# The first six output tiles: x stored early, and the last layer's bf16 result added onto it in DRAM by GpSimd's transfers

## The reference, cut to what matters

```python
x = x + L0_ffn(cond(x))   # ternary weights, 1024 hidden
x = x + L1_ffn(cond(x))   # mixture of experts, top 2 of 8
x = x + L2_ffn(cond(x))   # int8 weights, gate and up, 704 hidden
inputs = cond(x)          # last layer: sigmoid(x) * ratio
h = mx_layernorm(bf16_round(inputs)); h = mx_linear(h, W1, b1)
h = mx_gelu(h);                       h = mx_linear(h, W2, b2)
x = x + bf16_round(bf16_round(inputs) + h)
```

## Time and profile before

| | us |
|---|---|
| median of 3 runs | 413.33 (412.79 to 413.59) |
| profiled execution, its own time | 415.14 |
| its span | 413.4 |
| its mean granted TensorE clock | 0.963 of full speed |

### The profile page before, as it was taken

One profiled execution on the slowest core, in us unless ns is written; L12 is line 12 of the kernel. 1 busy time (PEld: TensorE's weight loads), 2 busy tenths in 40 slices (PEclk: granted clock), 3 DMA queues, 4 the chain that ended last, 5 costly groups with the idle time before them and its releaser, 6 DMA issues.

```text
span 413.4 us, 7058 instructions
## 1 busy us (share of the span) xinstructions
PE 365.5 (88%) x2496; PEld 314.6 (76%) x2507; DVE 337.5 (82%) x495; ACT 288.6 (70%) x513; POOL 90.7 (22%) x107
## 2 busy tenths in 40 slices
PE   3995458779789999999999999999998998999885
PEld 1995445458677889999999999999986787878453
DVE  4999966999885999999999980899404797899986
ACT  5999956996978378757667675766543455778873
POOL 4000300000030153343333332447530000000000
PEclk9998587989996999999999999999999999999999
DMA  7700000000048865411161279381004200000002
GB/s 274 262 2 2 1 0 0 2 0 2 1 131 300 287 195 168 174 39 40 34 246 40 74 273 367 77 304 43 25 27 131 88 0 2 1 2 2 0 27 78
DMA packets 22642, 38.41 MB, mean 93 GB/s; under 512 B 2072, under 2 KB 17064, under 8 KB 22480
## 3 DMA queue, kind: packets, MB, share of 16 engines
q1 hardware_dynamic: 17120, 24.98, 17.6%
q0 software_dynamic: 2480, 6.95, 5.0%
q10 hardware_dynamic: 3008, 6.03, 4.2%
HBM read 32.83 MB, written 5.11 MB: 92 GB/s over the span
## 4 chain that ended last, share of the span: by engine, by line
PE 65%; ACT 16%; DVE 11%; issue 5%; DMA 2%; SPq 0%; ACTq 0%; DVEq 0%
PE bank L1773 20%; PE bank L1813 19%; PE bank L1609 7%; PE bank L1892 3%; PE bank L1643 2%; PE bank L1882 2%; ACT big L494 1%; ACT big L493 1%; DVE big L1304 1%; ACT yT L558 1%; PE bank L1803 1%; DMA v<-in_kT 1%; DMA g<-choice_rows 1%; PE bank L1661 1%; ACT big L570 1%
## 5 line engine op out<-in xcount | busy, mean ns | idle before, releaser
L1813 PE MATMUL bank<-big,yT 128*128 (+1 forms) x368 | 83.6, 380 | 0.0
L639 ACT ACTIVATE yT<-bank,big 128x128 f32<-128x128 f32 x176 | 50.3, 368 | 41.7 <-PE bank L1773 41.7
L1813 PEld LDWEIGHTS bank<-big,yT 128*128 128x128 f32 x368 | 68.0, 190 | 8.7 <-issue 0.4
L392 POOL TENSOR_TENSOR small<-small 128x2 f32<-128x2 f32 (+1 forms) x9 | 9.6, 1071 | 167.9 <-DVE small L1339 71.1
L440 POOL DMA_INDIRECT choice_rows<-yo,rowo x23 | 30.5, 1325 | 61.5 <-ACT yo L648 48.8
L425 POOL DMA_INDIRECT xg<-token_rows,rowi x22 | 32.3, 1469 | 50.0 <-PE bank L1803 28.3
L1773 PE MATMUL bank<-ygT,w3T 128*128 128x128 f32 x256 | 30.2, 276 | 0.6 <-ACT ygT L631 0.6
L1773 PEld LDWEIGHTS bank<-ygT,w3T 128*128 128x128 f32 x256 | 29.8, 192 | 1.1 <-issue 0.7
L1773 PEld LDWEIGHTS bank<-ygT,big 128*128 128x128 f32 x256 | 29.8, 192 | 0.7 <-issue 0.4
L1773 PE MATMUL bank<-ygT,big 128*128 128x128 f32 x256 | 29.9, 275 | 0.0
L1773 PEld LDWEIGHTS bank<-ygT,y 128*128 128x128 f32 x224 | 26.0, 192 | 1.5 <-issue 1.2
(11 more groups left out here) (383 smaller groups left out, 823.8 us busy)
## 6 DMA issues: line engine op xcount, KB each, us to landing
big<-in_moe_w SPq DMA_DIRECT2D x16, 1024.0 KB
v<-in_kT SPq DMA_DIRECT2D x2, 512.0 KB, 4.5
big<-in_gateT SPq DMA_DIRECT2D x1, 1024.0 KB, 6.9
big<-in_upT SPq DMA_DIRECT2D x1, 1024.0 KB, 9.0
big<-in_downT SPq DMA_DIRECT2D x1, 1024.0 KB, 11.2
x<-in_x_bsc SPq DMA_DIRECT2D x1, 1024.0 KB, 13.6
token_rows<-y POOLq DMA_DIRECT2D x4, 256.0 KB, 7.9
ek<-in_w3a ACTq DMA_DIRECT2D x1, 1024.0 KB, 5.8
```

Source lines behind the costliest of these rows:

```text
L392: gp.tensor_tensor(dst, src, pexp[:, 0:dst.shape[1]], ALU.pow).then_inc(dst_sem, 1)
L639: ins = sc.activation(hT[j % 2][:, c], ps[1 + 2 * (j % 2) + c // 4][:, (c % 4) * P:(c % 4 + 1) * P], ACT.Gelu, bias=b1s[:, c, j:j + 1] if ...
L1813: ins = te.matmul(ps[5 + 2 * (j % 2)][:, 0:C], hT[j % 2][:, c], big[:, bass.ds(at + (W2_AT + c * C), C)] if j else big[:, W2_AT + c * C:W2 ...
```

## The change

VectorE no longer adds the bf16 sums of tiles 0 to 5 to x. SP stores x of each of the first three pairs, 256 KB at a time, when `x_l2` says that layer 2 has been added. When all three stores have landed, GpSimd's queue adds the bf16 sums of each pair onto the output in DRAM by a transfer with `accum_op=add`, from bf16 in SBUF to float32 in DRAM. Tiles 6 and 7 are finished and stored as before. `ob` becomes eight tiles, four of them in free columns of `big`, so ScalarE's waits for `x_done` go. SP waits at the end for the two plain stores and the three adding transfers. To stay within the number of semaphores, some that were always waited for together are merged (the waits ask for the sum of the counts).

```diff
@@ SP
-            for i in range(T):
-                sp.wait_ge(s["x_done"], i + 1)
+            for p in range(G - 1):
+                sp.wait_ge(s["x_l2"], p + 1)
+                sp.dma_start(out_v[:, 2 * p:2 * p + 2], x[:, 2 * p:2 * p + 2]).then_inc(s["x_out"], 16)
+            for i in (T - 2, T - 1):
+                sp.wait_ge(s["x_done"], i - T + 3)
                 sp.dma_start(out_v[:, i], x[:, i]).then_inc(s["stored"], 16)
-            sp.wait_ge(s["stored"], 16 * T)
+            sp.wait_ge(s["stored"], 32)
+            sp.wait_ge(s["sum_out"], 16 * (G - 1))
@@ GpSimd, behind the four powers
+            out_v = out.rearrange("b (s p) c -> p (b s) c", p=P)
+            pool.wait_ge(s["x_out"], 16 * (G - 1))
+            for p in range(G - 1):
+                pool.wait_ge(s["sum_ready"], p + 1)
+                gp.dma_start(out_v[:, 2 * p:2 * p + 2], ob_pair[p], accum_op=ALU.add).then_inc(s["sum_out"], 16)
@@ ScalarE
             def copy_ob(i):
                 act.wait_ge(s["d3_ready"], i + 1)
-                if i >= 4:
-                    act.wait_ge(s["x_done"], 2 * (i // 2) - 2)
-                sc.activation(ob[:, i % 4], ps[7][:, 0:C], ACT.Copy).then_inc(s["ob_ready"], 1)
+                sc.activation(ob[i], ps[7][:, 0:C], ACT.Copy).then_inc(s["ob_ready"], 1)
@@ VectorE
             def finish_sum(i):
                 dve.wait_ge(s["ob_ready"], i + 2)
-                mark("sum", ve.tensor_tensor(pair_of(ob, i % 4), pair_of(ob, i % 4), pair_of(res, i), ALU.add))
-
-            def finish_pair(i):
-                after("sum")
-                ve.tensor_tensor(pair_of(x, i), pair_of(x, i), pair_of(ob, i % 4), ALU.add).then_inc(s["x_done"], 2)
+                ve.tensor_tensor(ob_pair[i // 2], ob_pair[i // 2], res[:, i:i + 2], ALU.add).then_inc(s["sum_ready"], 1)
...
-            finish_pair(0)
...
-            finish_pair(2)
...
-            finish_pair(4)
@@ merged semaphores: ld_wgu and ld_wd; w3_copy and r3_copy; w3_copy2 and r3_copy2
```

More of the change, by code:

```diff
@@ L134, in bass_adaln_ffn_stack @@
         q3T = [big[:, 11776 + 512 * j:12288 + 512 * j].bitcast(BF16).rearrange("p (c t) -> p c t", c=HC3) for j in range(2)]
-        ob = big[:, 12800:13312].bitcast(BF16).rearrange("p (t c) -> p t c", t=4)
+        ob = [big[:, at:at + 512].bitcast(BF16).rearrange("p (t c) -> p t c", t=4)[:, j] for at in (12800, 15360) for j in range(4)]
+        ob_pair = [big[:, at:at + 256].bitcast(BF16).rearrange("p (t c) -> p t c", t=2) for at in (12800, 13056, 15360)]
         b1t = big[:, 13312:13824].bitcast(BF16)
@@ L218, in bass_adaln_ffn_stack @@
             table_ready rowo_ready xt_ready xt_copy h1_ready ld_b2
-            yo_ready ld_v1 ld_wgu ld_wd ld_x ld_router ld_l2 ld_l3rows consts iota_done
+            yo_ready ld_v1 ld_wgud ld_x ld_router ld_l2 ld_l3rows consts iota_done
             act_step dve_step pool_step tf_sum tf_ready tf2_ready decay_ready sx_ready ek_raw ek_ready ekv_ready clamped euk_ready
@@ L223, in bass_adaln_ffn_stack @@
             silu_ready z_ready sq2 amax2 rms2_in rms2_pow scale2 q2_magic q2_tr q2T_ready
-            down_ready q2T_last x_l0 sig1 yT_ready rh_ready rh_gelu logits lg_shift lg_exp last_gelu last_sum last_ps last_row  masks_ready             gate_ready gcT_tr gcT_ready ps1_ready ps2_ready bias_ready l1_done             w3q w3t w3_copy l2_int xt2_tr sig2 y2_ready y2h_ready y2T_ready gu2_ready silu2_ready h2_ready down2 x_l2             r3_tr r3_copy sig3 y3_ready var3 pow3 hq3 hq3_tr hq3T u3_ready a3_ready g3_ready q3_ready
-            q3_tr q3T_ready d3_ready ob_ready x_done stored w3_copy2 r3_copy2 bias_added br_ready b1_ready ld_b1 b1_turned b1s_ready w1_ready y1_stored a_ready b_ready rows_ps rows_ready ek_free zero_row""".split()
+            down_ready q2T_last x_l0 sig1 yT_ready rh_ready rh_gelu logits lg_shift lg_exp last_gelu last_sum last_ps last_row  masks_ready             gate_ready gcT_tr gcT_ready ps1_ready ps2_ready bias_ready l1_done             w3q w3t dve_copies l2_int xt2_tr sig2 y2_ready y2h_ready y2T_ready gu2_ready silu2_ready h2_ready down2 x_l2             r3_tr sig3 y3_ready var3 pow3 hq3 hq3_tr hq3T u3_ready a3_ready g3_ready q3_ready
+            q3_tr q3T_ready d3_ready ob_ready x_done stored act_copies bias_added br_ready b1_ready ld_b1 b1_turned b1s_ready w1_ready y1_stored a_ready b_ready rows_ps rows_ready ek_free zero_row sum_ready sum_out x_out""".split()
         s = {n: sem(n) for n in NAMES}
@@ L294, in _ @@
             for m, n in enumerate(("gateT", "upT")):
-                sp.dma_start(wgu[:, m], A[n].rearrange("(k p) h -> p k h", p=P)).then_inc(s["ld_wgu"], 16)
-            sp.dma_start(wd, A["downT"].rearrange("(c p) n -> p c n", p=P)).then_inc(s["ld_wd"], 16)
+                sp.dma_start(wgu[:, m], A[n].rearrange("(k p) h -> p k h", p=P)).then_inc(s["ld_wgud"], 16)
+            sp.dma_start(wd, A["downT"].rearrange("(c p) n -> p c n", p=P)).then_inc(s["ld_wgud"], 16)
             sp.dma_start(x[:], A["x_bsc"].rearrange("b (s p) c -> p (b s) c", p=P)).then_inc(s["ld_x"], 16)
@@ L513, in _ @@
             euk(1)
-            act.wait_ge(s["ld_wgu"], 32)
-            act.wait_ge(s["ld_wd"], 16)
+            act.wait_ge(s["ld_wgud"], 48)
             for m in range(3):
@@ L705, in _ @@
                 act.wait_ge(s["w3t"], b + 1)
-                sc.activation(w3T[:, 1, (b - 2) * 1024:(b - 1) * 1024], ps[b][:].bitcast(BF16), ACT.Copy).then_inc(s["w3_copy2"], 1)
+                sc.activation(w3T[:, 1, (b - 2) * 1024:(b - 1) * 1024], ps[b][:].bitcast(BF16), ACT.Copy).then_inc(s["act_copies"], 1)
             for b in range(2, 4):
                 act.wait_ge(s["r3_tr"], b + 1)
-                sc.activation(r3t[:, 2 * b:2 * b + 2].rearrange("p t c -> p (t c)"), ps[4 + b][:], ACT.Copy).then_inc(s["r3_copy2"], 1)
+                sc.activation(r3t[:, 2 * b:2 * b + 2].rearrange("p t c -> p (t c)"), ps[4 + b][:], ACT.Copy).then_inc(s["act_copies"], 1)
             for b in range(2):
@@ L1262, in _ @@
                 dve.wait_ge(s["w3t"], b + 1)
-                ve.tensor_copy(w3T[:, 0, b * 1024:(b + 1) * 1024], ps[b][:].bitcast(BF16)).then_inc(s["w3_copy"], 1)
+                ve.tensor_copy(w3T[:, 0, b * 1024:(b + 1) * 1024], ps[b][:].bitcast(BF16)).then_inc(s["dve_copies"], 1)
             for b in range(2):
                 dve.wait_ge(s["r3_tr"], b + 1)
-                ve.tensor_copy(r3t[:, 2 * b:2 * b + 2].rearrange("p t c -> p (t c)"), ps[4 + b][:]).then_inc(s["r3_copy"], 1)
+                ve.tensor_copy(r3t[:, 2 * b:2 * b + 2].rearrange("p t c -> p (t c)"), ps[4 + b][:]).then_inc(s["dve_copies"], 1)
             dve.wait_ge(s["br_ready"], 1)
@@ L1323, in norm_in @@
                 dve.wait_ge(s["sig3"], p + 1)
-                dve.wait_ge(s["r3_copy"], 2)
-                dve.wait_ge(s["r3_copy2"], 2)
+                dve.wait_ge(s["dve_copies"], 4)
+                dve.wait_ge(s["act_copies"], 4)
                 ve.tensor_tensor(pair(res, p), y3[p % 2], pair(r3t, p), ALU.mult).then_inc(s["y3_ready"], 1)
@@ L1452, in finish_sum @@
                 dve.wait_ge(s["ob_ready"], i + 2)
-                mark("sum", ve.tensor_tensor(pair_of(ob, i % 4), pair_of(ob, i % 4), pair_of(res, i), ALU.add))
-            def finish_pair(i):
-                after("sum")
-                ve.tensor_tensor(pair_of(x, i), pair_of(x, i), pair_of(ob, i % 4), ALU.add).then_inc(s["x_done"], 2)
+                ve.tensor_tensor(ob_pair[i // 2], ob_pair[i // 2], res[:, i:i + 2], ALU.add).then_inc(s["sum_ready"], 1)
             def tile_sum(i):
                 dve.wait_ge(s["ob_ready"], i + 1)
-                mark(("sum", i), ve.tensor_tensor(ob[:, i % 4], ob[:, i % 4], res[:, i], ALU.add))
+                mark(("sum", i), ve.tensor_tensor(ob[i], ob[i], res[:, i], ALU.add))
             def finish_tile(i):
                 after(("sum", i))
-                ve.tensor_tensor(x[:, i], x[:, i], ob[:, i % 4], ALU.add).then_inc(s["x_done"], 1)
+                ve.tensor_tensor(x[:, i], x[:, i], ob[i], ALU.add).then_inc(s["x_done"], 1)
             dve.wait_ge(s["ld_sgu"], 16)
@@ L1846, in _ @@
             ratio_to_tokens(3, 4, s["r3_tr"])
[L1848 to L1851, removed]
+            pe.wait_ge(s["dve_copies"], 4)
+            pe.wait_ge(s["act_copies"], 4)
             keep_clock(6, 7)
```

## The result

The changed kernel is slightly slower. On 20 runs its median is 415.53 us against 414.18 for the kernel before on the same chips, and the ratio is 1.003 (95% interval 1.0016 to 1.0045): 1.2 us more, where 0.4 us less was forecast. Its own profiled execution took 415.44 us, with a span of 413.7.

The account below looks back on a forecast made before the run. The prediction took the end to be bound by the chain of VectorE's last tile, one store and its landing. Its sum, -0.6 (second addition) + 0.2 (shared engines) = -0.4 us, took 413.33 to 412.9 us, range 412.3 to 415.2.

Parts of the forecast that it names:

- Step (2): Removing VectorE's addition for tiles 2 and 3 lets tile 7's maximum start 0.61 to 0.83 us earlier; taken as 0.6.
- The bound by TensorE: Clock-keeping matmuls ahead of TensorE's turn of tile 6 do not move, limiting that branch's gain to 0.64 us.
- Steps (1), (3) and (4): Removing VectorE's additions for tiles 0/1, for tiles 4/5, and ScalarE's four waits for x: each worth nothing.
- Early stores at nothing: SP's three added 256 KB stores of x cost nothing, covered by the empty DMA.
- The third transfer's latency: GpSimd's adding transfer for tiles 4 and 5: 4.8 us from issue to landing, landing at 412.5.
- The 0.2 us for shared engines: At the end, third adding transfer and last plain store finish together and share DMA engines, adding 0.2 us.
- So the end is this chain: VectorE's last tile, one store, a landing: End of the kernel before: last store issued 411.3, data down about 413.0 of a 413.4 us span.
- three signs of being wrong: Third landing over 6.2 us; SP's last wait for adding transfers by over 0.5 us; early stores shifting work before 399.
- Rival C: Third adding transfer becomes the end, deciding from 5.4 us latency, over 0.8 us slower from 6.2; chance 0.30.
- Rival D: VectorE holds up writing the third transfer's descriptors, making the time 413.5 us; chance 0.06.
- E: The second addition's place ahead of tile 7's maximum stays empty, so no gain, 413.5 us; chance 0.06.
- The 0.27 for "slower": Chance of over 0.2% slower: 0.25 from Rival C's larger part, 0.02 from Rival D and E.

Follow-up runs that it names:

- e8: Kernel before, with room for eight tiles of bf16 sums and the addition for tiles 2 and 3 moved behind tile 7's quantisation; ratio 0.997.
- e9: Kernel before plus the three early 256 KB stores of x, overwritten by the usual stores at the end; ratio 0.9995.
- e7: Changed kernel, but the third GpSimd transfer converts bf16 to float32 without adding, leaving x out of tiles 4 and 5; ratio 1.0002 to the kernel before.

## Why the prediction was wrong

- **Step (2), the gain, was right in mechanism and under-sized.** The maximum could start 0.03 us after the GELU, the upper end of the 0.61 to 0.83 given, and the whole chain moved by 0.8 us, not 0.6. The 0.36 us of "issue" at 401.48 did not stay: in the changed kernel VectorE was idle for 0.15 us at that place (400.35 to 400.50), most of it until the GELU was done, and in e8, where this addition comes long after its sum, nothing like it stands before it. (The addition there is that of tiles 2 and 3, the second, not "the first adding of x".) The bound by TensorE (0.64 us; its own figures, 405.51 - 404.85, give 0.66) failed, because the end of the clock-keeping matmuls that I took (403.82 + 1.03) is a modelled one; the turn started 0.16 us ahead of that end in the changed kernel (403.57 against 402.70 + 1.03).
- **Steps (1), (3) and (4) at nothing: right.** e8 keeps the additions of tiles 0/1 and 4/5 on VectorE and has the full gain. e8 drops ScalarE's waits and so does not test (4), but the rows bear it out: the eviction of tile 6 stood behind TensorE's product for 0.55 us in the kernel before and does so in the changed one.
- **Early stores at nothing: right** (e9).
- **The third transfer's latency was right as a number:** 4.8 us estimated between bounds of 2.4 and 8.1, 4.7 and 4.5 measured. Part of that is luck: it was the middle of two even rates, and the measured transfer began at 47 GB/s. Over all traces, adding transfers took 3.8 to 4.7 us, 3.8 to 4.6 with no store near them. The Trainium skill's fit (DMA: Bandwidth & Descriptors, Anatomy of one DMA) gives an estimate of 3.5 us for 640 KB, read and written bytes together; the measurement says more for an adding transfer. For e7, which only converts, the fit's estimate is 2.9 us for the 384 KB read and written and 2.6 us for the 256 KB written; the trace has 2.6.
- **The 0.2 us for shared engines was too small.** The last store landed in 2.4 instead of 1.7 us, so 0.7, and e7 shows that the adding does it. With this and the gain, SP was done 11.3 us after the GELU (411.8 - 400.47), against 11.4 before (413.0 - 401.59). Gain and sharing alone would have made no difference.
- **The step that failed is "So the end is this chain: VectorE's last tile, one store, a landing".** It gave the end 0.4 us behind the last landing, whatever queue that came from. GpSimd's own closing drain, 2.2 us behind the landing of its last transfer and at least 4.1 behind its last instruction, was not in the sum. It is now what ends the kernel: 413.5, 1.5 us behind SP's 412.0. None of the three signs of being wrong that the prediction named came up (the landing took 4.7 us, and SP's last wait for data was for the store): they watch landings, SP's waits and the stages before 399, not the drains.

The account: -0.8 (chain), +0.7 (last store slower), +1.5 (drain instead of SP) = +1.4 us, which is 13.2 - 11.8. Rival C had the right transfer at the end of the path, but let it decide only from 5.4 us of latency on and make the kernel clearly slower from 6.2. The landing was 4.7, before the last store's; the transfer decides all the same, because its landing is followed by 2.2 us of drain, and the last store's by 0.3 us of closing on SP (411.7 to 412.0). That mechanism no rival had. Rival D (VectorE holding up the descriptors) was not seen: the third issue took 1.19 us in runs with different work beside it. E did not occur. The 0.27 for "slower" was for the wrong reason. The 1.2 us lie inside the range given, which reached 1.9 us above the kernel before; the forecast missed the direction.

The drain was there to be read in the kernel before, in the rows of the closing line: 4.99 us from the start of a power of 0.86 us. "Who else must be done at the end, and how long does its last step take?" was the question not asked.

## What to carry to other kernels

Before work is given to GpSimd near the end of a kernel, add its closing drain: in these traces the kernel did not end sooner than about 4.1 us behind GpSimd's last instruction, nor 2.2 us behind the landing of its last transfer, and with GpSimd's last work 20 us ahead of the end this cost nothing. An adding transfer of 256 KB landed 3.8 to 4.7 us after issue, 1 to 2 us later than a plain one (2.9), and slowed plain stores beside it. When one instruction in front of the chain is the whole gain, look first for a place behind the chain on its own engine: moving the one addition (e8) gave 0.8 us with no transfer at all.

## What had not been expected of the hardware

GpSimd's closing DRAIN follows a rule that all the traces here fit: it ends at the later of about 4.1 to 4.4 us behind the end of its last instruction (power 387.69 to 391.8; memset 410.49 to 414.6; one-row store 412.31 to 416.5; converting transfer 408.84 to 413.2) and 2.2 us behind the landing of its last transfer (411.3 to 413.5; 412.25 to 414.5; 408.8 to 411.06). VectorE's, ScalarE's and TensorE's closing drains took 0.41 to 0.72 us, SP's 0.01. What GpSimd does in these 4 us is not shown by any row.
